# A preLN attention and FFN block: input tiles and a first Q slice moved into the last unit of each batch

## The reference

```python
x = x + attn(layernorm(x), Wq, bq, Wk, bk, Wv, bv)
x = x + einsum('bsi,oi->bso', layernorm(x), weight * scale_weight[:, None]) + bias
# attn: q, k, v per head; query block i of 128 attends to keys i*128-64 .. (i+1)*128+64 (softmax);
# rows 0, T-1 and the 62 queries of largest norm attend to all keys instead,
# and their results are written over those of the local attention
```

## Time and profile before

| | us |
|---|---|
| median of 3 runs | 2314.24 (2309.74 to 2315.69) |
| the profiled execution's own time | 2307.23 |
| its span, first to last instruction | 2305.7 |
| TensorE matmuls busy | 2198.3 (95%) |
| VectorE busy | 1520.1 (66%) |
| ScalarE busy | 818.1 (35%) |
| POOL busy | 602.8 (26%) |
| mean granted TensorE clock | 0.990 |

### The profile page before, as it was taken

One profiled execution on the slowest core, in us unless ns is written; L12 is line 12 of the kernel. 1 busy time (PEld: TensorE's weight loads), 2 busy tenths in 40 slices (PEclk: granted clock), 3 DMA queues, 4 the chain that ended last, 5 costly groups with the idle time before them and its releaser, 6 DMA issues.

```text
span 2305.7 us, 39651 instructions
## 1 busy us (share of the span) xinstructions
PE 2198.3 (95%) x13024; PEld 1864.1 (81%) x13024; DVE 1520.1 (66%) x3130; ACT 818.1 (35%) x2073; POOL 602.8 (26%) x468
## 2 busy tenths in 40 slices
PE   4999999989999999899999998999999987999999
PEld 3878888868788888787888887878888876888887
DVE  5587775663877755638777657297776567666664
ACT  2224444442244444522444445224444451000000
POOL 1232222223232231232322312324123123222211
PEclk9999999999999999999999999999999998999999
DMA  3221111112311111022111110231111103333331
GB/s 119 89 87 43 50 57 39 51 34 79 96 42 50 57 39 52 31 78 92 49 50 41 57 50 29 69 96 58 39 50 59 39 23 135 136 136 136 136 127 73
DMA packets 106434, 159.97 MB, mean 69 GB/s; under 512 B 9648, under 2 KB 75254, under 8 KB 106352
## 3 DMA queue, kind: packets, MB, share of 16 engines
q1 hardware_dynamic: 98416, 140.03, 18.6%
q10 hardware_dynamic: 4608, 16.78, 1.8%
q0 software_dynamic: 3328, 2.17, 0.5%
HBM read 107.53 MB, written 51.41 MB: 69 GB/s over the span
## 4 chain that ended last, share of the span: by engine, by line
PE 73%; DVE 16%; issue 6%; ACT 4%; DVEq 0%; DMA 0%; SPq 0%; ACTq 0%; another core or an unknown queue 0%; POOL 0%; POOLq 0%
PE proj L439 33%; PE proj L661 15%; PE pv L532 8%; PE turn L522 5%; PE score L507 3%; PE pv L577 3%; ACT probs L757 2%; DVE x_norm L1002 2%; DVE top_idx L1000 2%; DVE top_val L998 2%; PE score L558 2%; DVE neg_max L1047 1%; PE turn L652 1%; DVE q_sq L965 1%; DVE norms L967 1%
## 5 line engine op out<-in xcount | busy, mean ns | idle before, releaser
L439 PE MATMUL proj<-xT_hi,w_hi 128*128 128x512 f32 x1536 | 402.2, 404 | 4.9 <-DVE xT_lo L959 2.0
L439 PE MATMUL proj<-xT_hi,w_lo 128*128 128x512 f32 x1536 | 406.1, 397 | 0.0
L439 PE MATMUL proj<-xT_lo,w_hi 128*128 128x512 f32 x1536 | 382.1, 391 | 0.0
L439 PEld LDWEIGHTS proj<-xT_lo,w_hi 128*128 128x128 f32 x1536 | 289.0, 188 | 62.4
L439 PEld LDWEIGHTS proj<-xT_hi,w_lo 128*128 128x128 f32 x1536 | 283.0, 189 | 62.8
L439 PEld LDWEIGHTS proj<-xT_hi,w_hi 128*128 128x128 f32 x1536 | 275.8, 189 | 61.1 <-issue 4.7
L757 ACT ACTIVATE probs<-score,neg_max 128x256 f32<-128x256 f32 (+1 forms) x512 | 228.7, 459 | 263.2 <-DVE neg_max L1045 155.5
L334 POOL TENSOR_TENSOR ctx_out<-pv_sum,row_inv 128x256 f32<-128x256 f32 x128 | 88.2, 689 | 725.7 <-DVE pv_sum L1079 725.7
L326 POOL TENSOR_TENSOR w_lo<-w_raw,w_hi 128x1024 fp32r<-128x1024 f32 x98 | 242.4, 2473 | 7.9
L324 POOL CAST w_hi<-w_raw 128x1024 fp32r<-128x1024 f32 x98 | 107.5, 1097 | 493.8 <-PE proj L439 308.4
L1058 DVE TENSOR_TENSOR pT_lo<-turn,pT_hi 128x1024 fp32r<-128x1024 f32 x128 | 156.7, 1224 | 106.8 <-ACT pT_hi L769 100.6
(11 more groups left out here) (139 smaller groups left out, 3588.2 us busy)
## 6 DMA issues: line engine op xcount, KB each, us to landing
w_raw<-in_wstream SPq DMA_DIRECT2D x98, 512.0 KB, 3.8
q_store<-in_rows SPq DMA_DIRECT2D x36, 512.0 KB, 3.4
x_buf<-in_rows SPq DMA_DIRECT2D x36, 512.0 KB, 3.3
q_rows<-q_nat SPq DMA_DIRECT2D x64, 256.0 KB, 2.3
ctx_rows<-ctx_out SPq DMA_DIRECT2D x128, 128.0 KB, 1.8
q_store<-ctx_rows SPq DMA_DIRECT2D x32, 512.0 KB, 4.1
out<-q_store ACTq DMA_DIRECT2D x32, 512.0 KB, 2.6
bias_b<-in_bias_ffn SPq DMA_DIRECT2D x1, 512.0 KB, 7.5
```

What stands on the lines that cost most here:

```text
L439: mm = pe.matmul(proj[:, half, :], w[b][:, k * P:k * P + P], x[:, k, half * HALF:half * HALF + HALF], start=(m == 0), stop=(m == 23), skip ...
```

## The change

- TensorE: the filling work is named by 11 places `fill(0)` to `fill(10)` in a unit. In the first 7 units the 8 projection parts stand where they stood. In the last unit the eight tiles take `fill(0)` to `fill(7)`, which lie earlier: two between one turn of p and the next. In batches 1 to 3 `fill(8)` and `fill(9)` compute the two parts of the first half of the next batch's first Q slice, before and after `turn_gp`. The batch loop covers three batches, and the fourth stands behind it.
- ScalarE and VectorE read the tiles at places to match.
- VectorE, in all 32 units: `maxima` of step s+1 ahead of `p_lo_out` of step s.
- POOL: the wait for the scatters stands in the next batch, ahead of `load_columns`, not at the end of the batch.

```diff
-        LAST_TILES = [[0], [1], [2], [3], [4], [5], [6], [7]]
+        FILL_PART = {0: 0, 1: 1, 3: 2, 5: 3, 7: 4, 8: 5, 9: 6, 10: 7}
@@ POOL, batch loop
                 split(n, PAIRS + 2, 0, n * BUFS + PAIRS // 2 + 1)
+                pool.wait_ge(scattered, n * (16 * PAIRS))
                 load_columns(n, 0)
...
-                pool.wait_ge(scattered, (n + 1) * (16 * PAIRS))
@@ TensorE
-            def attend(n, hp, ahead):
+            def early_q(n, part):
+                if part == 0:
+                    for h in range(2):
+                        pe.wait_ge(xT_set[h], (n + 1) * TILES)
+                    apart(pe)
+                project_half(n, 0, 0, n * BUFS, 0, (part,))
+            def attend(n, hp, place):
...
+                def fill(k):
+                    if place == "ahead" and k in FILL_PART:
+                        m = FILL_PART[k]
+                        b = m // 4
+                        project_half(n, PAIRS + 2 + 2 * hp + b, b, n * BUFS + PAIRS // 2 + 1 + hp, (m // 2) % 2, (m % 2,))
+                    if place != "ahead" and k < TILES:
+                        if k == 0:
+                            pe.wait_ge(proj_free[1], at_k + 2)
+                        t = ROW_ORDER[k]
+                        turn_rows(last_rows if k == 0 else q_store[:, t, :], (n + 1) * TILES + k, proj_banks)
+                    if place == "next" and k >= TILES and k < TILES + 2:
+                        early_q(n + 1, k - TILES)
                 scores(u, 0, at_k)
                 turn_v(u, 0, at_v)
-                part(0)
+                fill(0)
                 turn_v(u, 1, at_v)
                 turn_p(u, 0)
                 scores(u, 1, at_k)
-                part(1)
+                fill(1)
                 turn_v(u, 2, at_v)
+                fill(2)
                 weigh(u, 0)
                 turn_p(u, 1)
                 scores(u, 2, at_k)
-                part(2)
+                fill(3)
                 weigh(u, 1)
+                fill(4)
                 turn_p(u, 2)
                 scores(u, 3, at_k)
-                part(3)
+                fill(5)
                 weigh(u, 2)
+                fill(6)
                 turn_gq(u)
                 turn_p(u, 3)
-                part(4)
+                fill(7)
                 global_scores(u)
                 weigh(u, 3)
-                part(5)
+                fill(8)
                 turn_gp(u)
-                part(6)
-                part(7)
+                fill(9)
+                fill(10)
                 global_weigh(u)
...
+            for part in range(2):
+                early_q(0, part)
+            with pe.Fori(0, BATCH - 1) as n:
+                batch(n, "next")
+            batch(BATCH - 1, "linear")
@@ ScalarE, attend
                 next_rows(1)
                 v_hi_out(u, 2)
+                next_rows(2)
                 pv_lo_out(u, 0)
                 p_hi_out(u, 1)
                 exps(u, 2)
-                next_rows(2)
+                next_rows(3)
                 pv_lo_out(u, 1)
+                next_rows(4)
                 p_hi_out(u, 2)
                 exps(u, 3)
...
@@ VectorE, attend
                 v_lo_out(u, 1)
+                maxima(u, 1)
                 p_lo_out(u, 0)
-                maxima(u, 1)
                 inverses(u, 0)
                 top_norms(1)
                 next_rows(1)
                 v_lo_out(u, 2)
+                next_rows(2)
                 pv_sums(u, 0)
+                maxima(u, 2)
                 p_lo_out(u, 1)
-                maxima(u, 2)
                 inverses(u, 1)
                 top_norms(2)
-                next_rows(2)
+                next_rows(3)
                 pv_sums(u, 1)
+                next_rows(4)
+                maxima(u, 3)
                 p_lo_out(u, 2)
...
```

More of the change, by code:

```diff
@@ L579, in global_weigh @@
                 mm.then_inc(pv_done, 1)
-            def attend(n, hp, ahead):
-                u = n * PAIRS + hp
-                def part(k):
-                    if not ahead:
+            def early_q(n, part):
[5 more added lines that the diff above has]
+            def attend(n, hp, place):
+                u = n * PAIRS + hp
+                at_v = n * SLICES + PAIRS + 2 * hp
+                at_k = at_v + 1
+                def fill(k):
[4 more added lines that the diff above has]
+                    if place != "ahead" and k < TILES:
                         if k == 0:
                             pe.wait_ge(proj_free[1], at_k + 2)
[L589 to L597, removed]
+                        t = ROW_ORDER[k]
+                        turn_rows(last_rows if k == 0 else q_store[:, t, :], (n + 1) * TILES + k, proj_banks)
+                    if place == "next" and k >= TILES and k < TILES + 2:
+                        early_q(n + 1, k - TILES)
                 scores(u, 0, at_k)
                 turn_v(u, 0, at_v)
-                part(0)
+                fill(0)
                 turn_v(u, 1, at_v)
@@ L608, in attend, with batch @@
                 scores(u, 2, at_k)
-                part(2)
+                fill(3)
                 weigh(u, 1)
+                fill(4)
                 turn_p(u, 2)
                 scores(u, 3, at_k)
-                part(3)
+                fill(5)
                 weigh(u, 2)
+                fill(6)
                 turn_gq(u)
                 turn_p(u, 3)
-                part(4)
+                fill(7)
                 global_scores(u)
                 weigh(u, 3)
-                part(5)
+                fill(8)
                 turn_gp(u)
-                part(6)
-                part(7)
+                fill(9)
+                fill(10)
                 global_weigh(u)
[L626 to L632, removed]
+            def batch(n, place):
                 with pe.Fori(0, PAIRS // 4) as j:
@@ L643, in _ @@
                 with pe.Fori(0, PAIRS - 1) as hp:
-                    attend(n, hp, True)
-                attend(n, PAIRS - 1, False)
+                    attend(n, hp, "ahead")
+                attend(n, PAIRS - 1, place)
+            for t in range(TILES):
+                turn_rows(q_store[:, t, :], t, (proj_banks, turn_banks)[t % 2], 2)
+            for part in range(2):
[3 more added lines that the diff above has]
+            batch(BATCH - 1, "linear")
             def turn_lin(t, b):
@@ L791, in next_rows @@
                     if not ahead:
-                        for i in LAST_TILES[k]:
-                            rows_hi((n + 1) * TILES + i, ROW_ORDER[i], proj_banks)
+                        rows_hi((n + 1) * TILES + k, ROW_ORDER[k], proj_banks)
                 v_hi_out(u, 0)
@@ L813, in attend @@
                     v_out(n, hp + 1, 1)
-                next_rows(3)
+                next_rows(5)
                 pv_lo_out(u, 2)
+                next_rows(6)
                 gq_hi_out(u)
                 p_hi_out(u, 3)
-                next_rows(4)
+                next_rows(7)
                 global_exps(u)
@@ L1103, in next_rows @@
                     if not ahead:
-                        for i in LAST_TILES[k]:
-                            rows_lo((n + 1) * TILES + i, ROW_ORDER[i], proj_banks)
+                        rows_lo((n + 1) * TILES + k, ROW_ORDER[k], proj_banks)
                 def top_norms(k):
@@ L1123, in attend @@
                 v_lo_out(u, 2)
+                next_rows(2)
                 pv_sums(u, 0)
+                maxima(u, 2)
                 p_lo_out(u, 1)
-                maxima(u, 2)
                 inverses(u, 1)
                 top_norms(2)
-                next_rows(2)
+                next_rows(3)
                 pv_sums(u, 1)
+                next_rows(4)
+                maxima(u, 3)
                 p_lo_out(u, 2)
-                maxima(u, 3)
                 inverses(u, 2)
@@ L1155, in attend @@
                     row_roots(n, hp + 1, scale_c[:, bass.ds(hp, 1)])
-                next_rows(6)
-                if ahead:
                     row_normalise(tile)
                     k_lo_out(n, hp + 1, 1)
-                next_rows(7)
                 g_out(n, u, hp)
```

4 lines of the change are left out of this document (removed).

## The result

The changed kernel takes 2325.56 us (median of 5 runs, 2321.78 to 2328.5) against 2310.95 before (5 runs, 2309.74 to 2315.69): ratio 1.0057, 95% interval 1.0041 to 1.0074. It is slower by 14.6 us. The forecast was 2312.2 with a range to 2321, so it was wrong; the time is that of the third rival, at 2325, in part by luck (see the point-by-point account). The profiled run took 2321.78 us with a span of 2320.2, at a mean granted clock of 0.983 (before 0.990).

What follows compares the result with a forecast made beforehand. TensorE's own work was taken to bound the kernel nearly everywhere, with slack in each batch's last unit. Terms -10.2 + 3.0 + 4.8 + 0.4 = -2.0 us against the 2314.24 median gave 2312.2 us, range 2302 to 2321.

Steps and rivals of the forecast that it cites:

- the third rival: Last units: clock falls in every step, three stretches each, 18 us; with -7.2 that is +10.8, 2325. Chance 0.11.
- The waits: Last unit's steps: second tile waits 3.8 us, turn of p 2.9 later, then cycles of 7.55 against 6.68.
- A 3 us stretch costs at most 1.5 us of work ... 1.2 x 4 = +4.8: Last units: half clock after the 3.8 us idle costs 1.2 us in each of four units, +4.8.
- +0.4 for the short idles: Other steps of the last units: 0.3 us a unit for shorter idles, less 0.8 already lost in the third batch.
- With the same gap of 1.14 at the loop's end: TensorE's batch end: gap stays 1.14 us, so the second Q half starts at 513.0 instead of 516.41.
- the forecast's sum is -7.2: Whole kernel without clock terms: -10.2 for the earlier Q slice in three batches, +3.0 for the fourth batch.
- Rival 4: Batch starts: late third Q slice or a code gap takes about 1 us a batch; +1, 2315. Chance 0.07.
- The early half slice: End of last units in three batches: 3.4 us gained each after all delays, -10.2.
- Fourth batch, +3.0: Linear part's start: the 4.5 us delay comes through via loads behind the context stores, 1.5 taken back.
- Maxima 0: VectorE in the other 28 units: p_lo stays hidden by some 0.3 us, so the order costs and gains 0.
- POOL's wait -1.5: Linear part: without the scatter wait add_bias starts 1.50 us earlier, ending TensorE's 1.67 us wait; 1.5 back.
- POOL's split and SP: Third Q slice's split on POOL hidden with 2.8 us to spare; SP's next load some 15 us early; both 0.

Runs made afterwards that it cites:

- experiment 1: Changed kernel plus useless matmuls (14, 5 and 5) filling three TensorE waits of each last unit, nothing reordered: 2309.48 us, ratio 0.9993.
- experiment 2: Changed kernel plus only the 14 useless matmuls in the idle ahead of the third tile of each last unit: 2311.95 us, ratio 1.001.
- experiment 3: Changed kernel with ScalarE's high parts of each step's first tile ahead of that step's exponentials, last unit only: 2310.4 us, ratio 1.0005.
- experiment 4: Changed kernel with TensorE's loop over the first three batches written out: 2313.61 us, ratio 1.0016.
- experiment 5: Changed kernel with the useless matmuls of experiment 1 and TensorE's batch loop written out: 2295.69 us, ratio 0.9939.
- experiment 10: Kernel of experiment 9 with TensorE's batch loop written out: 2280.18 us with SP's first linear-part loads ahead of the last two context stores, 2280.13 us without.
- Experiment 6: Changed kernel with the first half of each first Q slice back at the batch's start, tiles still two per step: 2340.36 us, ratio 1.0119.
- experiment 7: Kernel before with only the maxima of step s+1 ahead of p_lo of step s, all 32 units: 2313.68 us, ratio 1.0006.
- experiment 9: Kernel of experiment 3 with VectorE's low parts ahead of the maxima again in the last unit and the third tile behind the first weighing: 2291.54 us, ratio 0.9909.
- experiment 8: Kernel before with only POOL's wait for the scatters moved ahead of load_columns: 2309.49 us, ratio 0.9988.
- experiment 11: Kernel of experiment 10 with early loads, plus 30 and 13 useless matmuls around the first turn of x_norm: 2280.51 us, ratio 0.9864.

## Why the prediction was wrong, point by point

- **The waits: right.** Second tile idle 3.8, measured 3.57; turn of p +2.9, measured +2.85 with the clock held (14.06 - 11.21 from the unit's start, experiment 1); cycle 7.55, measured 7.43 to 7.58; end of the unit 43.3, measured 43.4.
- **"A 3 us stretch costs at most 1.5 us of work ... 1.2 x 4 = +4.8", with +0.4 for the short idles: the step that failed.** The clock's part is 16.4 us by experiment 1, not 5.2. I had one stretch of 3 us a unit; the trace shows one or two of 6.8 to 10.2 us in each. Read in pieces of half a microsecond, the granted clock is under 1.00 for 20.5, 13.7, 13.7 and 27.3 us in the four last units with what follows them up to the slice or into the linear part (before: 3.4, 3.4, 10.2, 17.1, of which 13.7 in the linear part's start). Over the run, its last 3 us left out, it is 78.5 us (before 44.4, experiment 1 47.8). So the profiled executions of the change and of experiment 1 differ by 30.7 us of half clock and by 12.1 us of time (2321.78 and 2309.73): 0.39 us for each, and the forecast's 1.2 for 3 us is 0.40. Over all runs the median mean clocks, 0.979 and 0.990, make it about 51 us of half clock for the 16.4, 0.32 each. The price of half clock was about right; how much of it there would be was wrong. I had reasoned that idles shrink at half clock; they hardly did: 1.42 and 1.35 us stayed ahead of the weighings (1.48 and 1.40 in experiment 2, where the clock held), and TensorE came from one slow stretch into the next. The trace of before could have warned me: beside the stretch of the earlier trace rows the clock fell to 0.50 in the steps twice more, at 1427.0 to 1430.0 in batch 3 and 1881.0 to 1884.0 in batch 4, in units whose steps have no idle over 1.13 us.
 That was rival 3, which I gave 0.11. Its sum was +10.8 on a base of 2314.24; measured are +14.6 on 2310.95. That both come to 2325 is luck: its 18 us for the clock are near the 16.4, but its -7.2 for the rest leaves out the loop's end.
 The Trainium skill (TensorE: Matmul & The Clock Gate, Why this matters for your kernels) asks for no idle gap above about 3 us between bursts. The trace agrees for the 3.57 us idle. Shorter idles are not safe either: the clock fell behind the 2.20 us idle in one batch of four in experiment 3, and behind one of 1.47 us in experiment 2. The prediction told the rule without its length; the 1.92 us idle that it names as agreeing is such a shorter one.
- **"With the same gap of 1.14 at the loop's end": the second failure.** It is 2.70 and 3.39 us in batches 1 and 2, with half clock behind it. Before, TensorE's last semaphore wait was for the last tile, some 5 us ahead of the loop's end with a tile's turns and the global weighing behind it, and the gap seen was 1.14, 0.42 and 0.32. After, the last wait is that of the global weighing, only 2.4 us long. In both, from about that release to the next batch's first matmul it takes 5 to 6 us. For before, that time counts from the last tile's turns (5.92, 5.35 and 5.19 us from the first of them, the wait for their second half a little later); for after, from the global weighing's start (5.10 and 5.80). That reading is an inference from the traces; that the gap belongs to the loop's jump is shown, for it is 0 where the loop is written out and where the third batch leaves the loop. Without the clock's terms the forecast's sum is -7.2; experiment 1, clock held in the units, has -1.8. Of the 5.4 between them its gaps are 2.99 + 3.13 + 0 - 3 x 1.14 = 2.7; what half clock behind them and the fourth batch add was not told apart. Experiments 4, 5 and 10 value the whole jump at 11.0 to 12.7 us. Rival 4 had a gap at the batch's start, at 1 us a batch.
- **The early half slice: right in sign.** Experiment 6 gives 15.2 us where 8 to 12 were expected, half clock counted in.
- **Fourth batch, +3.0: short, and its reason is wrong.** Measured +7.24 to the first turn of x_norm and 1.2 back behind it. Experiments 1 and 5 have 52.95 and 51.99 from the unit's start to that turn against 47.70: 4.3 to 5.3 us without half clock in the steps (but with some in the global step), where the forecast had 4.5; the rest is clock. The loads of the linear part do not carry it. VectorE's addition of x and the attention's result follows the last unit's global result (g_ctx), which stands ahead of it in VectorE's order. VectorE's timeline before, after, and with early loads (experiment 10):

```profile
1909.91 0.25 DVE L1094 TENSOR_SCALAR g_ctx<-g_sum,row_inv 128x64 f32<-128x64 f32 x1
...
1925.60 0.25 DVE L1108 TENSOR_SCALAR g_ctx<-g_sum,row_inv 128x64 f32<-128x64 f32 x1
1926.14 1.22 DVE L1221 TENSOR_TENSOR q_store<-x_buf,q_store 128x1024 f32<-128x1024 f32 x1 [0.29 <-issue]
...
1881.60 0.25 DVE L1115 TENSOR_SCALAR g_ctx<-g_sum,row_inv 128x64 f32<-128x64 f32 x1
1882.15 1.23 DVE L1233 TENSOR_TENSOR q_store<-x_buf,q_store 128x1024 f32<-128x1024 f32 x1 [0.29 <-issue]
```

 The addition starts 0.54, 0.54 and 0.55 us behind g_ctx, in the last case 21.5 us after its loads were issued, and TensorE's idle before the first turn is 7.74 us each time. So the delay of the global weighing comes through whole, by VectorE's chain and not by a load.
- **Maxima 0 and POOL's wait -1.5: right in total.** From the first to the second turn of x_norm it takes 12.5 us instead of 13.7, so 1.2 of the 1.5. The cover of some 0.3 us in the other 28 units held (419.11 against 419.39). What I had not asked is what the order does to the last units' clock (experiment 7).
- **POOL's split and SP: hidden, as forecast.** The rest of each batch takes as long as before within 0.9 us, but for batch 2 with +2.24, where the clock was low at its start (988.5 to 996).

## What to carry to other kernels

An idle of the engine whose clock follows its activity has two prices, the idle itself and the work at half clock behind it, and where short waits follow, the second repeats: read the granted clock by short windows through the whole stretch, and price a bad case as all of it, not one stretch. When two instructions are moved apart to fill slack, look first at the buffer pair between them: in experiment 9 the same filling work, in an order without the long wait on that pair and with the low parts of p first again, is worth 33.6 us more, and in experiment 3 a shorter wait alone 15.4. As far as the traces tell, a loop's jump costs what the work queued behind the engine's last semaphore wait doesn't cover, so a change of the last block changes it.

## What the runs showed of the hardware

- Useless matmuls in three waits of a unit, done four times, gained 16.4 us of 2326 (experiment 1).
- Long half clock behind one idle: 3.57 us idle, then 8.00 us at 0.50 with TensorE busy all the time (478.50 to 486.50). The second stretch, 490.50 to 496.50, was busy throughout as well. Both are mostly turns and weighings; whether it is the kind of matmul that keeps the clock low wasn't isolated.
- In the changed kernel the next batch's first matmul starts 5.10 and 5.80 us after the start of the global weighing where TensorE's loop goes round, and 2.25 us after it, without idle, where the loop is written out (experiments 4 and 5). With the half clock behind it, writing the loop out gave 11.0 to 12.7 us for two jumps.
- The clock is not settled by the length of one idle: it held behind 2.20 us in three batches and fell in the fourth (experiment 3), fell once in four batches behind 1.4 to 1.5 us (experiment 2), and fell three times in before's steps with no idle over 1.13 us.
- A VectorE operation on 128x1 elements takes 2.27 to 3.30 us while POOL adds 128x1024 elements from SBUF, and 0.16 to 0.19 otherwise. In three kernels (before, experiments 8 and 11) it ends within 0.03 us of POOL's two additions.
